# Row maxima twelve key-tile steps ahead of the shifted scores instead of sixteen, with their transposition at the sixth step of the head ahead

## What is computed

```python
q = (x @ Wq + bq).reshape(b, n, H, DK)          # H = 8 heads, DK = 32
k, v = ...                                      # in the same way
logits = einsum('bhnd,bhmd->bhnm', q, k) / sqrt(DK)
logits = logits + log(clip(adj, 1e-8))          # third layer
logits = logits + (2 * adj - 1)                 # fourth layer, whose weights are
                                                # multiplied by (0.25 + 0.75 * adj)
attn = softmax(logits, axis=-1)
out = einsum('bhnm,bhmd->bhnd', attn, v) @ Wo + bo
```

## Time and profile before

| | us |
|---|---|
| median of 3 runs | 4452.08 |
| lowest and highest run | 4448.81, 4457.96 |
| the profiled execution | 4446.08 |
| its span, first to last instruction | 4444.3 |
| mean granted clock of TensorE | 0.957 |

### The profile page before, as it was taken

How to read it: one execution, slowest core, us unless ns; L and a number is a source line. 1 busy time by engine, 2 the same in 40 slices (tenths; PEclk the granted TensorE clock), 3 DMA queues, 4 the chain that set the end, 5 groups by cost and what they waited for, 6 DMA issues and landing times.

```text
span 4444.3 us, 69344 instructions
## 1 busy us (share of the span) xinstructions
PE 4062.8 (91%) x21040; PEld 2185.1 (49%) x21040; DVE 3042.6 (68%) x5152; ACT 2204.3 (50%) x3894; POOL 1917.8 (43%) x1064
## 2 busy tenths in 40 slices
PE   7998999989999899998999989998999989999898
PEld 6534465344753447543474434744347443574335
DVE  3797746877478764787647876478755787557874
ACT  3365533655336553365534655246543465435663
POOL 1174602746027560265503655036540465404562
PEclk9998999999999999999999999999999999999999
DMA  3201102011020110201112011120111101111010
GB/s 107 77 18 34 51 21 67 18 34 51 25 63 18 34 51 30 60 15 37 48 31 60 16 37 48 34 57 14 39 48 37 53 13 39 50 38 50 11 41 15
DMA packets 106289, 176.57 MB, mean 40 GB/s; under 512 B 27296, under 2 KB 50336, under 8 KB 105888
## 3 DMA queue, kind: packets, MB, share of 16 engines
q1 hardware_dynamic: 105888, 171.69, 13.5%
HBM read 83.12 MB, written 8.39 MB: 21 GB/s over the span
## 4 chain that ended last, share of the span: by engine, by line
PE 58%; issue 15%; POOL 15%; DVE 7%; ACT 3%; SPq 1%; DMA 1%; POOLq 0%; DVEq 0%; ACTq 0%
POOL region_p L1455 11%; PE ps L706 11%; PE ps L565 9%; PE ps L573 9%; PE ps L625 7%; PE ps L675 7%; PE ps L654 7%; PE ps L792 4%; PE ps L614 2%; POOL rstd L1465 1%; SPq L475 1%; DVE region_p L1226 1%; POOL y_t L1516 1%; DVE sums_t L1148 1%; DMA region_k<-region_p 1%
## 5 line engine op out<-in xcount | busy, mean ns | idle before, releaser
L1455 POOL TENSOR_TENSOR region_p<-region_p,mask 128x1024 f32<-128x1024 f32 x608 | 1444.7, 2391 | 427.7 <-ACT region_p L920 426.7
L1196 DVE TENSOR_REDUCE row_max_bf<-ps 128x1 bf16<-128x1024 f32 x768 | 938.9, 1224 | 152.2 <-PE ps L675 133.5
L706 PE MATMUL ps<-region_p,shelf 128*64 128x512 f32 x3584 | 942.8, 597 | 7.8 <-ACT o_raw L943 5.1
L920 ACT ACTIVATE region_p<-ps 128x512 f32<-128x512 f32 x1216 | 660.2, 595 | 407.2 <-PE ps L654 406.3
L654 PE MATMUL ps<-region_q,region_k 97*64 97x512 bf16 x4096 | 685.7, 395 | 2.8
L675 PE MATMUL ps<-region_k,region_q 96*64 96x512 bf16 x3584 | 585.9, 394 | 8.6 <-DVE row_max_bf L1192 8.6
L1182 DVE TENSOR_TENSOR region_p<-ps,mask 128x512 f32<-128x512 f32 x832 | 529.8, 680 | 57.1 <-ACT ps L916 56.6
L1465 POOL TENSOR_TENSOR rstd<-var_eps,minus_half 128x2 f32<-128x2 f32 (+1 forms) x160 | 116.9, 731 | 982.7 <-DVE var_eps L1128 982.7
L916 ACT ACTIVATE ps<-ps 128x512 f32<-128x512 f32 x832 | 446.0, 580 | 178.4 <-PE ps L654 170.2
L654 PEld LDWEIGHTS ps<-region_q,region_k 97*64 97x64 bf16 x4096 | 254.4, 111 | 403.5 <-DVE region_p L1182 129.0
L675 PEld LDWEIGHTS ps<-region_k,region_q 96*64 96x64 bf16 x3584 | 200.4, 112 | 425.9 <-issue 386.8
(11 more groups left out here) (160 smaller groups left out, 5355.5 us busy)
## 6 DMA issues: line engine op xcount, KB each, us to landing
mask<-in_adj SPq DMA_DIRECT2D x64, 512.0 KB, 7.0
mask<-in_adj_t SPq DMA_DIRECT2D x64, 512.0 KB, 3.4
y_t<-o_raw SPq DMA_DIRECT2D x224, 64.0 KB, 2.0
sums_t<-o_raw SPq DMA_DIRECT2D x224, 64.0 KB, 2.0
region_q<-region_p SPq DMA_DIRECT2D x192, 64.0 KB, 2.0
region_k<-region_p SPq DMA_DIRECT2D x192, 64.0 KB, 2.0
region_q<-sums_t SPq DMA_DIRECT2D x192, 64.0 KB, 2.0
region_k<-sums_t SPq DMA_DIRECT2D x192, 64.0 KB, 2.0
```

Source lines behind the costliest of these rows:

```text
L706: last = nc.tensor.matmul(ps[64 * c:64 * c + 64, VALUE_BANK, :], values_and_one, probs[:, t % RING, c * HALF:(c + 1) * HALF], start=(t == ...
L920: nc.scalar.activation(probs[:, t % RING, c * HALF:(c + 1) * HALF], scores_t, ACT.Exp, scale=DK ** -0.5).then_inc(exp_done, 1)
L1196: nc.vector.tensor_reduce(row_max_bf[i][:, t:t + 1], flat[:, (t % 2) * N:(t % 2 + 1) * N], AX.X, ALU.max)\
L1455: nc.gpsimd.tensor_tensor(p, p, mask[:, t, :], ALU.mult).then_inc(masked_pool, 1)
```

## The change

Maxima run AHEAD = 12 steps ahead instead of 16. A function later(h, t) says whose maximum stands in step t of head h: the tile twelve steps on. So only tiles 0 to 3 of head 1 are left as lead steps; its tiles 4 to 7 stand in steps 0 to 3 of head 0, as plain reductions, and everything after them four steps later than before. The last four maxima, tiles 4 to 7 of head 7, stand in steps 0 to 3 of head 6. The transposition of the next head's maxima moves from step 2 to step 5 (ROWS_AT), and SP issues the row of maxima of a head behind the four moves of o_raw instead of ahead of them. VectorE's tiles become 1, 3, 6 in heads 0 to 5 and 1, 3, 6, 7 in head 6 (0, 2, 4, 6 before). The late banks start with tile 6 of head 6 instead of with head 6.

```diff
+AHEAD = 12
+ROWS_AT = 5
 RING = 4
-POOL_TILES = {h: (0, 1, 2, 4, 6) for h in range(H - 2)}
-POOL_TILES[H - 2] = (1, 3, 5, 7)
+POOL_TILES = {h: (0, 2, 4, 5, 7) for h in range(H - 2)}
+POOL_TILES[H - 2] = (0, 2, 4, 5)
 POOL_TILES[H - 1] = (1, 3, 4, 6)
...
-LEAD_TILES = {h: tuple(range(T)) for h in range(2)}
+LEAD_TILES = {0: tuple(range(T)), 1: tuple(range(AHEAD - T))}
...
+def later(h, t):
+
+    at = h * T + t + AHEAD
+    return (at // T, at % T) if at < H * T else None
...
-            if t == 2 and h < H - 1:
+            if t == ROWS_AT and h < H - 1:
                 order.append(("rows", h + 1))
...
-        late = item[0] == "scores" and item[1] >= H - 2 and item[2] in DVE_TILES[item[1]]
+        late = (item[0] == "scores" and item[1] * T + item[2] >= H * T - AHEAD + 2
+                and item[2] in DVE_TILES[item[1]])
...
                     for h in range(H):
-                        if h + 2 < H:
-                            max_row(h + 2)
                         if h == H - 1:
                             sp.sem_inc(o_moved[1], 64)
                             continue
...
+                        if h + 2 < H:
+                            max_row(h + 2)
...
             def head(b, layer, h):
...
-                    if t == 2 and h < H - 1:
+                    if t == ROWS_AT and h < H - 1:
                         rows_of_maxima(b, layer, h + 1)
-                    if h < H - 2:
-                        scores_for_maximum(b, layer, (0, h + 2), t)
+                    nxt = later(h, t)
+                    if nxt is not None:
+                        scores_for_maximum(b, layer, (0, nxt[0]), nxt[1])
...
                 head_loaded(b, layer, 1)
-                for t in range(T):
+                for t in range(AHEAD - T):
...
-                    if h < H - 2:
-                        maximum(b, layer, (0, h + 2), h % 2, t)
+                    nxt = later(h, t)
+                    if nxt is not None:
+                        maximum(b, layer, (0, nxt[0]), nxt[0] % 2, nxt[1])
```

More of the change, by code:

```diff
@@ L910, in head @@
                         take_sums(b, layer, h - 1)
-                    take_lead(b, layer, h + 2, t)
                     for c in range(2):
```

## The result

The changed kernel takes 4424.54 (median of four runs, 4418.61 to 4428.38) where the kernel before takes 4451.12 (four runs, 4448.81 to 4457.96): 0.9941 of it, 95% interval 0.9928 to 0.9953. I had forecast 4485, slower, with a range from 4436. The direction was wrong and the time lies under the range. The profiled execution took 4428.38 with a span of 4426.6, 17.7 less than before; for the changed kernel the profiled execution was the slowest of the four runs, for the one before it was quicker than each of its runs, so the two profiles show 17.7 of the 26.6.

A forecast was written before the change was run, and what follows sets the result against it. TensorE was taken to bound the middle heads, VectorE the starts and ends. Per graph -6.0 (start) + 7.75 (end) + 2.4 (wait in head 6) = +4.15, times 8 = +33: 4479 profiled, 4485 median, +0.7%, range 4436 to 4528.

The forecast's parts named there:

- What bounds each stretch: Whole kernel: starts wait for VectorE, TensorE is full in middle heads, VectorE is full from head 6 to head 7's values.
- The shortened start: Lead steps and head 0: 9.0 a graph gained at full clock, 6.0 with the clock still falling; ends 4.4 and 9.0.
- the last of the signs of being wrong that I had named: Starts of the layers: the forecast is wrong if they keep full clock in most graphs.
- The rule of the Trainium skill: Starts: avoid long idle gaps to keep the clock up; by it the gain would be 9.0 in place of 6.0.
- The middle heads: Middle heads: new tiles, later transposition and later row cost zero, with ±0.15 a head, ±12 over 80 heads.
- The longer end: Head 6 to head 7's values: four reductions in VectorE's queue cost 7.75 a graph, ends 7.25 and 8.15.
- The new wait in head 6: Step 4 of head 6: TensorE idle 2.3 for a bank, then half clock; 2.4 a graph, ends 0 and 4.6.
- The sum: All terms: -6.0 + 7.75 + 2.4 = +4.15 a graph, +33 in all; median 4485, 6.0 above the profile.
- rival (a): Start and new wait in head 6: the clock holds, -1.25 a graph, 4442; no change, chance 0.20.

The follow-up runs named there:

- before_fill: The kernel before with twelve unread matmuls added in the waits of the lead steps, three in each of four waits: 4421.37, 0.9935 of the kernel before.
- late_quarters: The changed kernel with the four quarters of the inversion in head 6 at steps 3, 4, 5, 7 in place of 1, 3, 5, 7: 4462.02.
- before_plus: The kernel before with the scores for the maximum of two tiles of head 4 made twice in layer 0: 4467.25.
- lead16_rest: The changed kernel with maxima sixteen steps ahead again (AHEAD = 16), all else of the change kept: 4426.81.

## Why the prediction was wrong, step by step

**What bounds each stretch: right.** The starts wait for VectorE, the middle heads are TensorE's, the ends VectorE's queue. Every stretch at full clock came out within 0.3 a head, and a little over 1 at the end.

**The shortened start: the mechanism right, the clock wrong, and this is the step that failed.** I laid the changed start out at 3.13 + 14.15 = 17.28; it takes 16.98, since the wait in step 4 ends 7.12 after head 0 begins and not 7.46 (1309.73 against 1302.61). Then I wrote that the changed start "still has such a run" of waits, "so I expect the fall to stay, with 6.8 at half clock", and took off 1.5 a layer. The clock held in 11 starts of 16 in one profile and in 14 in the other, which is the last of the signs of being wrong that I had named; where it fell, the mean granted clock of the 17.2 was 0.90, so that it was at half for 3.4, and that cost 0.2 to 0.3. Gain: 9.6 a graph (76.7 by 8) where I had 6.0. The falls of the kernel before were in its times already: the 14.17, 14.96 and 4.20 that I took for full clock hold them, and at full clock before_fill has 13.54 and 13.55 for head 0. What I had to ask was whether half as long a run of waits still brings one, and I answered by the sort of the waits and not by their number. The runs with sixteen, fourteen and twelve steps and the same tiles show that the number counts: 16, 9, and 5 or 2 falls.

Of the 9.6, at full clock 20.63 - 16.98 = 3.65 a layer, 7.3 a graph, is the lead steps' own time less what head 0 grew by, and 2.3 is the price of the falls that they had brought, as before_fill measures it.

The rule of the Trainium skill that I had set against the trace did not settle it either. By the Trainium skill, "TensorE: Matmul & The Clock Gate", "Why this matters for your kernels", neither start would have fallen, and before it fell 15 times in 16. The same page of the Trainium skill, "A second HAM failure mode: psum-queue depth-cycling", tells of a kernel whose TensorE was idle for short moments between groups of matmuls so often that its clock went up and down; with that the starts of before agree, and it was the place to look.

**The middle heads: right.** 933.8 for 933.9. The tiles, the transposition at step 5 and the later row of maxima cost nothing there.

**The longer end: right in kind, 1.25 a graph too high.** At full clock heads 5 and 6 up to head 7's values grew by 3.2 in layer 0 (35.94 for 32.74) and 3.3 in layer 1 (34.55 for 31.25), 6.5 a graph where I had 7.75. In layer 1 I had 21.0 for VectorE's queue and 19.95 is measured; 0.87 of the difference is the scaling, which I took at 2.1 from the earlier trace rows and which took 1.23 here:

```profile
1596.62 1.23 DVE L1375 TENSOR_TENSOR y_t<-y_t,sums_t 128x1024 f32<-128x1024 f32 x1
```

And head 7's values waited last for ScalarE's copy there (0.68), not for VectorE as I had said, by some tenths; in layer 0 they wait for it as before (2.07).

**The new wait in head 6: there, but its price too high.** It is 1.73 long and ends 9.3 after the head's start; I had 2.3 and 9.7. I charged 1.2 a layer for a clock fall after it in every layer. It fell in five layers of sixteen, 1.4 to 1.5 each, 0.9 a graph in place of 2.4. Again I took one fall after one long wait in the rows of before for a rule.

**The sum.** Per graph -9.6 + 6.5 + 0.9 = -2.2, by 8 -17.6, where I had -6.0 + 7.75 + 2.4 = +4.15, +33. Of the 50 between them the clock in the starts is about 23, the clock in head 6 is 12, the queue at the end 10, the start's layout 5. Then I set the median 6.0 above the profile, as it was in the kernel before; here it lay 3.8 below. My rival (a), that the clock holds, had the mechanism for most layers; its 4442 was too high by the same layout, queue and offset.

**What the change is worth without the clock.** -7.3 + 6.5 = -0.8 a graph, some 6 in all, under what a measurement here can tell. The two kernels with the falls filled out of the starts of before and out of head 6 of the change agree with that: their three stretches add up to 1775.5 and 1769.8, and the medians are 4421.37 and 4419.80. What stays open is the rest: it runs from 2624.8 to 2651.0 in kernels whose instructions there are the same (late_quarters aside), and which of its falls a kernel gets I can't tell beforehand.

## What to carry to other kernels

Price a change twice, at full clock and with the clock's falls, and look at the falls of the kernel before as a cost that the change may remove: a run of short waits can be filled with matmuls that nobody reads, which here brought 28 of 4450 (24 between the two profiles, 20 of them in the filled stretch itself), without a change to the schedule. Work moved from one crowded stretch to another gains little; here, put where the engine that paces both has room (one reduction in each of four middle heads), it left start and end both short. Differences of half a per cent between kernels of this kind should be followed to the stretches where they arise before a part of the edit gets the credit.

## What the runs showed of the chip that I had not expected

**A VectorE product of two SBUF tensors and a GpSimd product exclude each other.** The scaling of the output reads two SBUF tensors, 128 by 1024. It took 1.23 in the changed kernel, 2.17 before, 3.36 in late_quarters. GpSimd's products beside it, in the kernel before and then in the changed kernel, layer 1:

```profile
1603.75 2.36 POOL L1455 TENSOR_TENSOR region_p<-region_p,mask 128x1024 f32<-128x1024 f32 x1 [0.21 <-ACT region_p L920]
1606.34 3.09 POOL L1455 TENSOR_TENSOR region_p<-region_p,mask 128x1024 f32<-128x1024 f32 x1 [0.23 <-ACT region_p L920]
```

```profile
1589.77 4.68 POOL L1465 TENSOR_TENSOR region_p<-region_p,mask 128x1024 f32<-128x1024 f32 x2 [2.51 <-ACT region_p L929]
1597.08 3.01 POOL L1465 TENSOR_TENSOR region_p<-region_p,mask 128x1024 f32<-128x1024 f32 x1 [2.63 <-ACT region_p L929]
```

Before, GpSimd's product ends at 1606.11 and the scaling, begun at 1605.02, ends 1.08 later; in late_quarters the product ends at 1610.83 and the scaling, begun at 1608.55, again 1.08 later. In the changed kernel GpSimd was idle when it began. The product that starts during the scaling pays in turn: 3.09 and 3.01 in place of 2.36. So each waits for the whole instruction of the other, and a duration read from one place doesn't hold for another. The Trainium skill, "SBUF — State Buffer", "SBUF: two separate sides", says just that for a VectorE instruction with two SBUF inputs against a GpSimd one that reads SBUF: an exclusive lock for the whole instruction, no sharing. The trace agrees: the 1.08 stands in all sixteen layers of both kernels, and in the changed kernel the scaling takes 1.22 or 1.23 in all of its own. VectorE's mask products, which read PSUM and SBUF, are not held up: the one in the earlier trace rows, at 1367.80, took its 1.28 for two halves beside this one of GpSimd's, and of all the halves in the kernel before, those beside a GpSimd product and the 40 others both take 0.68 in the mean:

```profile
1366.38 2.36 POOL L1455 TENSOR_TENSOR region_p<-region_p,mask 128x1024 f32<-128x1024 f32 x1 [0.54 <-ACT region_p L920]
```

**Stretches with the same instructions differ by up to 3.3 a graph.** From head 7's values of one graph to the next graph's transposition it is 244.0 to 247.3 in the kernels with maxima sixteen steps ahead (before, before_fill, before_plus, lead16_rest; first and last graph aside), and in the pair looked at above the places with the half clock make the difference; the repeated graphs of a kernel have them mostly at the same places, which is why the difference does not average out over eight graphs.
